# Three loaded bands and nine split tiles where there were four and eight, in six products of a 4096 x 4096 matrix

## The reference, cut to what matters

```python
u = x
for _ in range(3):
    v = mlp(adj @ u, uv_W1, uv_b1, uv_W2, uv_b2, uv_W3, uv_b3)   # leaky_relu after each layer
    u = mlp(adj @ v, vu_W1, vu_b1, vu_W2, vu_b2, vu_W3, vu_b3)
x = layernorm(x + v)
x = layernorm(x + adj @ (x @ weight))
```

## Time and profile before

| | |
|---|---|
| Median of 3 runs | 1169.3 us (1168.79 to 1169.54) |
| The profiled execution | 1169.6 us, its span 1167.7 us |
| PE, DVE, ACT busy | 1150.3 us (99%), 742.9 (64%), 707.1 (61%) |
| Granted TensorE clock, mean | 0.999 of full speed |
| Moved by DMA | 281.4 MB, 241 GB/s on average |
| Loads of bands | 261 of 1 MB, median 5.1 us from issue to landing |

### The profile page before, as it was taken

How to read it: one execution, slowest core, us unless ns; L and a number is a source line. 1 busy time by engine, 2 the same in 40 slices (tenths; PEclk the granted TensorE clock), 3 DMA queues, 4 the chain that set the end, 5 groups by cost and what they waited for, 6 DMA issues and landing times. The chain is left out here.

```text
span 1167.7 us, 13986 instructions
## 1 busy us (share of the span) xinstructions
PE 1150.3 (99%) x5296; PEld 958.1 (82%) x5296; DVE 742.9 (64%) x871; ACT 707.1 (61%) x883; POOL 4.2 (0%) x12
## 2 busy tenths in 40 slices
PE   7999999999999999999999999999999999999997
PEld 6788888888888888888888888888887788888886
DVE  6976545554765454775564486554558875449997
ACT  6876544555675444765554486554567865458785
POOL 0000000000000000000000000000000000000000
PEclk9999999999999999999999999999999999999999
DMA  9987665645845566666653585655657564458894
GB/s 352 401 329 264 231 242 216 252 156 188 342 180 196 201 256 248 231 242 248 216 192 144 210 322 203 226 182 214 246 188 287 216 239 169 190 196 358 337 351 178
DMA packets 39361, 281.42 MB, mean 241 GB/s; under 512 B 4416, under 2 KB 4800, under 8 KB 5632
## 3 DMA queue, kind: packets, MB, share of 16 engines
q1 hardware_dynamic: 38736, 278.69, 63.4%
q0 software_dynamic: 560, 1.84, 0.4%
HBM read 278.41 MB, written 2.10 MB: 240 GB/s over the span
## 5 line engine op out<-in xcount | busy, mean ns | idle before, releaser
L630 DVE TENSOR_TENSOR low<-raw,high 128x1024 fp32r<-128x1024 f32 x522 | 609.0, 1217 | 42.4 <-ACT high L499 42.1
L872 PE MATMUL acc<-high,p_low 128*128 128x512 f32 x1544 | 604.2, 391 | 3.2 <-DVE low L630 3.2
L872 PE MATMUL acc<-high,p_high 128*128 128x512 f32 x1544 | 599.3, 388 | 0.0
L872 PE MATMUL acc<-low,p_high 128*128 128x512 f32 x1544 | 599.2, 388 | 0.0
L499 ACT ACTIVATE high<-raw 128x1024 fp32r<-128x1024 f32 x522 | 523.3, 1053 | 89.4 <-PE acc L872 56.2
L872 PEld LDWEIGHTS acc<-high,p_low 128*128 128x128 f32 x1544 | 290.1, 188 | 63.8 <-DVE low L630 6.0
L872 PEld LDWEIGHTS acc<-low,p_high 128*128 128x128 f32 x1544 | 289.9, 188 | 59.7
L872 PEld LDWEIGHTS acc<-high,p_high 128*128 128x128 f32 x1544 | 290.1, 188 | 57.8
L672 DVE TENSOR_TENSOR h_low<-h,h_high 128x512 fp32r<-128x512 f32 x40 | 27.7, 692 | 130.5 <-ACT h L535 130.5
L667 DVE TENSOR_TENSOR h<-acc,part 128x512 f32<-128x512 f32 (+1 forms) x37 | 24.9, 672 | 103.9 <-issue 63.9
L534 ACT ACTIVATE h_high<-h,consts 128x512 fp32r<-128x512 f32 x28 | 20.2, 721 | 107.8 <-DVE h L667 107.8
(11 more groups left out here) (53 smaller groups left out, 292.5 us busy)
## 6 DMA issues: line engine op xcount, KB each, us to landing
raw<-adj_dram SPq DMA_DIRECT2D x261, 1024.0 KB, 5.1
resid<-x_dram SPq DMA_DIRECT2D x1, 2048.0 KB, 11.6
out_dram<-part POOLq DMA_DIRECT2D x7, 256.0 KB, 5.1
resid<-x_turned_dram SPq DMA_DIRECT2D x2, 512.0 KB, 4.9
resid<-x_turned_dram SPq DMA_DIRECT2D x1, 1024.0 KB, 7.3
consts<-consts_dram SPq DMA_DIRECT2D x1, 464.0 KB, 7.1
out_dram<-part SPq DMA_DIRECT2D x2, 128.0 KB, 1.7
w_first<-first_dram SPq DMA_DIRECT2D x1, 64.0 KB, 1.8
```

Source lines behind the costliest of these rows:

```text
L630: nc.vector.tensor_tensor(low[t % SLOTS][:], raw_of(t), high[t % SLOTS][:].bitcast(F32), ALU.subtract).then_inc(low_ready, 1)
L872: done = nc.tensor.matmul(bank[:, into], p[parity][:, at:at + D], a[slot][:, columns], start=(n == s.opens and j == 0 and m == 0), stop=(n ...
```

## The change

- `RAWS` 8 to 6 (three buffers of bands), `SLOTS` 8 to 9, `AHEAD` 6 to 7. The space in SBUF is the same.
- The first weight and the turned `x` come from one array; the weight arrives with the first piece of `x`. One transfer and one semaphore less.
- `X_SPLIT`: p's chunks 0 to 2 are split ahead of tile 0, and chunks 3, 4, 5, 6, 7 ahead of tiles 1, 2, 3, 4 and 6.
- `NORM_TURN` 5 to 6: the turn of the fifth product and all that follows from it, one place later.
- The order of some buffers in SBUF.

```diff
-RAWS = 8
-SLOTS = 8
-AHEAD = 6
+RAWS = 6
+SLOTS = 9
+AHEAD = 7
...
-X_SPLIT = [0, 0, 0, 0, 0, 0, 2, 4]
+X_SPLIT = [0, 0, 0, 1, 2, 3, 4, 6]
...
-TURN, NORM_TURN = 8, 5
+TURN, NORM_TURN = 8, 6
...
-        w_first = sbuf("w_first", [D, D])
-
-        sbuf("pad", [D, D])
         w = {name: consts[:, bass.ds(i * D, D)] for i, name in enumerate(WEIGHTS)}
-        w[FIRST] = w_first[:]
...
-        resid = sbuf("resid", [D, N])
+        sbuf("pad", [D, D])
+
+
+        input_and_weight = sbuf("input", [D, D + N])
+        w[FIRST] = input_and_weight[:, 0:D]
+        resid = input_and_weight[:, D:D + N]
...
             def load_x(piece):
-                of_piece = bass.ds(sum(X_PIECES[:piece]) * CHUNK, X_PIECES[piece] * CHUNK)
-                sp.dma_start(resid[:, of_piece], x_turned[:, of_piece]).then_inc(x_loaded[piece], 16)
+                columns = slice(D + sum(X_PIECES[:piece]) * CHUNK if piece else 0, D + sum(X_PIECES[:piece + 1]) * CHUNK)
+                sp.dma_start(input_and_weight[:, columns], x_turned[:, columns]).then_inc(x_loaded[piece], 16)
...
-            sp.dma_start(w_first[:], first).then_inc(first_loaded, 16)
...
-                pe.wait_ge(first_loaded, 16)
+                pe.wait_ge(x_loaded[0], 16)
...
-    x_turned = put("x_turned_dram", _np.asarray(inputs["x"]).T)
+    x_turned = put("x_turned_dram", _np.concatenate([_np.asarray(inputs[_NAMES[FIRST]]),
+                                                     _np.asarray(inputs["x"]).T], axis=1))
```

More of the change, by code:

```diff
@@ L266, in place_banks, with gnn_kernel @@
             holder[s.bank] = i
-def gnn_kernel(nc, adj, x_turned, x_nodes, first, constants, out):
+def gnn_kernel(nc, adj, x_turned, x_nodes, constants, out):
     plan = Plan()
@@ L319, in gnn_kernel @@
         x_loaded = [sem(f"x_loaded{i}") for i in range(len(X_PIECES))]
-        first_loaded = sem("first_loaded")
         consts_loaded = sem("consts_loaded")
@@ L448, in load_x @@
             def load_x(piece):
-                of_piece = bass.ds(sum(X_PIECES[:piece]) * CHUNK, X_PIECES[piece] * CHUNK)
-                sp.dma_start(resid[:, of_piece], x_turned[:, of_piece]).then_inc(x_loaded[piece], 16)
+                columns = slice(D + sum(X_PIECES[:piece]) * CHUNK if piece else 0, D + sum(X_PIECES[:piece + 1]) * CHUNK)
+                sp.dma_start(input_and_weight[:, columns], x_turned[:, columns]).then_inc(x_loaded[piece], 16)
             def load_residual():
                 sp.wait_ge(x_projected, CHUNKS)
-                sp.dma_start(resid[:], x_nodes).then_inc(residual_loaded, 16)
+                sp.dma_start(resid, x_nodes).then_inc(residual_loaded, 16)
             def load(t):
@@ L913 @@
     adj = put("adj_dram", adj.transpose(0, 2, 4, 3, 1).reshape(CHUNKS, CHUNKS, D, IN_BAND * TILE))
-    x_turned = put("x_turned_dram", _np.asarray(inputs["x"]).T)
+    x_turned = put("x_turned_dram", _np.concatenate([_np.asarray(inputs[_NAMES[FIRST]]),
+                                                     _np.asarray(inputs["x"]).T], axis=1))
     x_nodes = put("x_dram", _np.asarray(inputs["x"]).reshape(N // D, D, D).transpose(1, 0, 2).reshape(D, N))
-    first = put("first_dram", inputs[_NAMES[FIRST]])
     columns = [_np.asarray(inputs[_NAMES[k]]) for k in WEIGHTS]
@@ L922 @@
     out = nc.dram_tensor("out_dram", (CHUNKS, D, CHUNK), F32, kind="ExternalOutput").ap()
-    gnn_kernel(nc, adj, x_turned, x_nodes, first, constants, out)
+    gnn_kernel(nc, adj, x_turned, x_nodes, constants, out)
     r = _run(nc, [arrays], core_ids=[0])
```

## The result

| | before | changed |
|---|---|---|
| Median, 5 runs each, side by side | 1169.54 us (1168.79 to 1170.88) | 1192.01 us (1190.07 to 1192.55) |
| Ratio | | 1.018, 95% interval 1.0166 to 1.0193 |
| Span of the profiled execution | 1167.7 us | 1190.2 us |
| PE busy | 1150.3 us (99%) | 1158.6 us (97%) |
| ACT waits for the landing of a band | 32.9 us, 40 times | 138.7 us, 109 times |

1178.0 was forecast, with a range to 1184. The sign was right, and so was the chain of waits that it gave for the first layers. The size was not: most of the loss lies in the last product, where the forecast had put 3 us.

A forecast was written before the change was run, and what follows sets the result against it. TensorE, busy 99% of the span, was taken as the bound. First layers with start and turn 0 +5.8, products 2 to 4 +1.5, fifth -1.5, last +3.0: +8.8 on 1169.6, 1178.4; forecast 1178.0 us for the median, range 1171.5 to 1184.0.

The forecast's parts named there:

- the chain of waits that it gave for the first layers: First layers: band landing, tile 18 raised, weights lowered, tile 17 lowered, next landing, tile 22 raised, layer 1, h_low: 15.8 us.
- Start: Start of the kernel: first visit 1.6 us earlier, given back in small waits over visits 2 to 6; net -0.3 us.
- First layers: First layers, the costliest place: PE waits 6.8 us, 2 of them at visit 17, against 1.5 before; +4 to +7.5.
- The sign that was named: First layers: PE idle of 4 us or more ahead of the first layer-2 matmuls near 44 us would show it right.
- The 0.8 us at turn 0: First layers: layer 3's ACT step stands behind tile 28, so turn 0 is late by another 0.8 us.
- Starts of products 2 to 4: Single-use tiles at these starts: third layer and next layer 2 late, +0.5 us each, +1.5 for three; 0 to +3.
- Fifth product: Turns one visit later: wait at turn 35 goes, -1.5 us; turn 33 nets 0; sum -1.5, between -3.2 and 0.
- Last product: Last product: less lead with three buffers, waits of 4.9 us against 1.9 before; +3.0 us, from -1 to +6.
- The turnaround: Buffer loop with DVE free: landing 4.7, raise 1.06, hand-overs 0.1, two tiles lowered 2.35: 8.2 us for three bands.
- Rival (c): All single-use stretches starve: other DVE and ACT work makes 9.5 us per three bands against PE's 8.5; 1184 to 1190; chance 0.12.
- Range: Whole kernel: 1171.5 (first layers +4, full turn gain, no loss behind) to 1184.0 (+7.5, and +6 in the last product).
- 1.5 per chunk over four chunks: Last product: the basis given for the upper bound of +6 us on its loss.

The follow-up runs named there:

- two-bank run: The changed kernel with the last product's projects writing in turn to two PSUM banks, proj and the first layer bank: 1190.51 us, ratio 1.0159.

## Why the prediction was wrong in size and right in kind

*Start.* Forecast: the first visit 1.6 us earlier, given back over visits 2 to 6. It was 2.2 earlier; 0.8 was given back by visit 6, and the rest up to visit 16, since bands 6 and 7 also came just late (0.78 and 0.60 us at visits 12 and 14). Net -0.43 against -0.3.

*First layers.* Forecast 6.8 us of waiting, 2 of it at visit 17; measured 1.25 there, 3.54 and 0.67 at layer 2, 1.38 at visits 12 and 14 just ahead. On the forecast's own footing, from the start of visit 13 to h_low, PE waited 6.5 us against 6.8: the chain was right in its steps and its size. (The sign that was named, 4 us or more ahead of the layer-2 matmuls, came just short: 3.38 and 0.51 by the records.) The sum by visits, 6.74, lies 0.6 above the forecast, and that it is so near is luck in part. The 0.8 us at turn 0 did not come (no wait is on record between 48.80 and 316.36 us), and 1.6 us of low clock that the forecast did not have stands in its place (last section).

*Starts of products 2 to 4.* 0.7, 0.6 and 1.6 us where 0.5 each was said, twice the sum but within its range, and mostly at the place that was said (turns at 316.36, 509.22 and 702.65 waited 0.6, 0.5 and 1.1).

*Fifth product.* -1.23 against -1.5: right, with the parts a little off. Turn 33 waited 0.6 where 0.9 was said and layer 2 ahead of it 1.2 where 0.6 was said.

*Last product.* The step that failed is "Followed tile by tile: ... 4.9 against 1.9 before. + 3.0". The turnaround was taken as 8.2 us "with DVE free", 1.37 per tile, with 4.7 in it for the landing. It was 10.6: landings of 5.4 on average and 5.2 us from landing to lowered where 3.5 stood in the sum. In that product DVE's finishing, adding and measuring of a chunk falls between the landing and the lowering of a band for 20 of the 29 bands (1.2 us on average over all), ACT's part of it too (1.0 us), and a turnaround has no slack to take it. PE's waits up to the last tile came to 13.9 us where 4.9 was said, against 1.9 before as said; another 1.6 us is low clock behind one of them. Rival (c) had the mechanism (9.5 us per three bands) and was given 0.12; it was the true one for this product, and with 10.6 even its price was low by a third of a microsecond per band. Its total, 1184 to 1190, came from fifteen turnarounds at 9.5 and lies under the 1192 measured too.

I also overlooked a consumer. The prediction compares tiles with visits, and never DVE's addition of a chunk with the next chunk's project. The two-bank run shows that this omission caused little of the miss: without the wait nearly the same time is lost at the tiles.

*Range.* The two ends were put together from terms taken one by one, with +6 for the last product. The lower end does not add up as described (+4 and -3.2 give 1170.1 and not 1171.5), which has no bearing on the miss. The bound "1.5 per chunk over four chunks" had no row behind it. From rows it would have been 28 bands x (3.5 - 3.0).

## What to carry to other kernels

Buffers that are filled by one engine's request and freed by another's work form a loop: landing, everything that stands in the consumers' programs up to the release, then the next request. Its time over the number of buffers must stay under the pace of the bound *with all other work of the consumers in it*, not with the consumer free; each microsecond that the loop is too long is paid once per turnaround. When memory is short, make buffers finer before making them fewer: six tile buffers lost 0.5% where three band buffers of the same memory lost 1.8% (both in the changed kernel), and eight in the kernel before gained 0.2%. And the longest new wait in a list need not be the cause: take it away and see whether the time moves.

## What the runs showed of the hardware that was not expected

After an idle stretch TensorE's granted clock can fall. Of the changed kernel, stretches of one microsecond (busy us of PE, PEld, DVE, ACT, POOL; then the clock, DMA share, GB/s):

```profile
1116.00:1117.00 1.00, 0.00 (x0) 0.00 (x0) 1.00 (x2) 0.58 (x1) 0.00 (x0) 1.00 1.10 467
...
1118.00:1119.00 1.00, 1.00 (x7) 1.00 (x7) 1.00 (x7) 0.51 (x2) 0.00 (x0) 0.50 0.57 205
1119.00:1120.00 1.00, 1.00 (x4) 0.84 (x4) 1.00 (x2) 1.00 (x2) 0.00 (x0) 0.50 0.99 418
```

PE had been idle for 2.66 us and then ran at 0.50 of full speed, 1.2 of 2.4 GHz, for some 3.4 us (the clock reads 0.92, 0.50, 0.50, 0.50 and 0.87 in the five microseconds from 1117): four matmuls in a microsecond where before and later there were six. The same stands behind the 3.5 us ahead of the first layer 2: visit 19 took 2.28 us (49.14 to 51.42) and visit 20 2.06 where 1.36 is normal, 1.6 us more. Behind idle stretches of 3.04 us (1095.50) and 2.52 us (1142.83) the clock stayed at 1.00, while with two banks it fell to 0.50 behind the idle stretch of 1.92 us at 1129.20. So a long wait can cost half as much again as it shows, and not each one does; the length of the idle stretch alone does not decide it, and what does was not tried.

Landings of 1 MB spread from 4.6 to 8.6 us in these two kernels with at most four in flight, leaving out the first bands (up to 14.8) and one of 11.7 right behind the 2 MB load of `x` in the kernel before. The band asked for at 1080.5 in the changed kernel landed 7.9 us later, while in the last two microseconds of it the transfer engines were busy for 0.30 and 0.23 of the time:

```profile
1087.00:1088.00 1.00, 1.00 (x9) 0.91 (x8) 0.53 (x1) 0.00 (x0) 0.00 (x0) 1.00 0.30 123
1088.00:1089.00 1.00, 1.00 (x6) 0.82 (x5) 0.00 (x0) 0.57 (x1) 0.00 (x0) 1.00 0.23 66
```

One more band, asked for at 1083.1, was on its way then. The view gives only the mean of the 16, so whether a few of them lagged or all went slowly is not shown, nor why.
